# Weighting a mixture of experts at its inputs instead of its outputs, with one PSUM accumulator, in a two-layer transformer kernel

## The chip, the cores and the metric

The kernel runs on one core of a Trainium2 chip. A core has TensorE (PE, matrix multiplies into PSUM), VectorE (DVE), ScalarE (ACT, activation functions and copies), GpSimd (POOL) and SyncE (SP, which here only issues DMAs). SBUF is the working memory of 128 partitions. PSUM has eight banks of 128 partitions x 512 float32. The engines run at their own pace and wait on semaphores. The metric is the device time of one execution in microseconds (us), lower is better.

## What is computed

Two layers on `x` of 16 sequences x 256 tokens x 128 features. The first adds a linear-kernel attention and a two-deep local-attention network. The second, the one that the change is about, adds a 16-head softmax attention and a mixture of 8 experts with a shared one:

```python
xn = _layernorm(x)
x = x + _L1_attn_ref(xn, Wk, bk, Wq, bq, Wv, bv, Wo, bo) + _L1_ffn_ref(xn, ...)

# _L1_ffn_ref: E = 8 experts, K = 2 chosen, H = 256
logits = jnp.einsum('bsd,de->bse', x, Wr) * SCALE
_, idx = jax.lax.top_k(logits + rb, K)
w = jax.nn.softmax(jnp.take_along_axis(logits, idx, axis=-1), axis=-1)
w_full = jnp.sum(jax.nn.one_hot(idx, E, dtype=x.dtype) * w[..., None], axis=-2)
h = jnp.einsum('bsd,edh->bseh', x, W1) * jax.nn.silu(jnp.einsum('bsd,edh->bseh', x, W3))
expert_out = jnp.einsum('bseh,ehd->bsed', h, W2)
out = jnp.einsum('bsed,bse->bsd', expert_out, w_full)
hs = jnp.einsum('bsd,dh->bsh', x, Ws1) * jax.nn.silu(jnp.einsum('bsd,dh->bsh', x, Ws3))
return out + jnp.einsum('bsh,hd->bsd', hs, Ws2)
```

Both kernels compute all eight experts for every token; `w_full` is zero where an expert was not chosen.

## The kernel before

All weights are loaded once (`block.sync`). Then eight turns run, each on two sequences (T = 512 tokens). Most tiles are feature-major: 128 features on the partitions, 512 tokens along the row. Every engine has its own hand-written instruction list, and the order within a turn is the order of that list.

A turn: layer norm; first layer; `x1` (token-major) is its result; a second layer norm (`norm`, DVE) gives `xn`; four transposes and an ACT copy give `xn2T`. From there, which is called the second part of the turn below:

- PE multiplies `xn2T` by the query and key weights (L739), the router weights `wr` (L743, eight small passes) and the value weights (L749).
- Queries and keys are split in three bfloat16 parts (ACT L932, POOL L429, ACT L934, POOL L431), stored to DRAM (`dparts`, SP L367) and read back, rearranged, by 26 DMAs (`qst`, `kst`; SP L373, L378). The semaphore `stack_in` tells that they have landed.
- DVE adds a bias to the values (`avz`, L1192) and then works out the router's top-2 weights `wf` in some 25 small, linked steps (L1203 to L1229), with an Exp on ACT in their midst (L937).
- PE computes experts. `expert_in(e)` makes four 128x512 products (L773 gates with `mw3`, L776 units with `mw1`). ACT applies Silu to the gates (L942), and DVE multiplies (`expert_hidden`, L1241) into `mh`. `expert_out(e)` multiplies `mh` by `mw2` in eight 128x128 pairs of passes (L765) into a PSUM bank of its own. DVE then adds it to `moe`, each token times its weight (`expert_add`, four instructions, L1252).
- Three experts run ahead of the wait for `stack_in` (`EARLY = 3`). Then 16 pairs of heads have their score maxima taken (PE L791 into `att_max` banks, DVE L1262), with one expert after every third pair (`EXPERT_AT`). The negated maxima (L1269, L1270) are transposed (PE L802), copied by ACT (L945) and sent through DRAM into `qst` (SP L382, L386; semaphore `nm_in`).
- Meanwhile PE computes the shared expert's gates and units (`expert_in(EX)`). Then come the scores (L817), 32 Exps on ACT (L955) and the value products (L833).
- At the end DVE divides (L1276, L1278), PE runs the output projection and the shared expert's `mw2` products into one bank (`final`, L763, L765), DVE adds `moe` (L1282), and SP stores `res`.

PSUM banks are given out at build time by `job(name, k, freed_by, count)`, in the order of PE's list. Ring `short` goes round banks 0 to 5, `long` holds 6 and 7. `freed(name)` is the wait for the last user of the bank. DVE's linked steps (`link`) each wait for the one before. `rsqrt` (L1003 to L1012) is a bit trick and three Newton steps of four linked instructions. It runs six times a turn: in both layer norms, and in each of the two local layers once on 64 columns (`loc_rs`) and once for its own layer norm (`glu_rs`).

## Time and profile before

| | |
|---|---|
| median of 3 runs (lowest to highest) | 2773.8 us (2756.99 to 2775.79) |
| the profiled execution's own time | 2776.88 us |
| its span, first to last instruction | 2774.7 us |
| mean granted TensorE clock | 0.872 |
| busy: PE / DVE / ACT / POOL | 73% / 50% / 25% / 8% of the span |
| chain that ended last, by engine | PE 58%, DVE 23%, DMA 6%, ACT 5% |

The profile is one execution. Its chain of work is followed back from the last instruction, at each step to what released it. A wait "<- X" is idle time that ended when X finished. The granted clock is 1.00 at 2.4 GHz and 0.50 at 1.2 GHz; a mean between them is a mix of both. A matmul on float32 stands in the trace as two passes, so "x2" is one product.

### The profile page before, as it was taken

How to read it: one execution, taken by the hardware profiler on the slowest of the kernel's cores; microseconds unless marked ns; L12 is line 12 of the kernel's file. 1: busy time of each engine (PE TensorE's matmuls, PEld its weight loads, DVE VectorE, ACT ScalarE, POOL GpSimd, SP SyncE). 2: the span in 40 equal slices, each digit the busy share in tenths (PEclk: the TensorE clock that was granted, in tenths of full speed). 3: DMA queues.
4: the chain of work that ended last, by engine and by line, in shares of the span. 5: the costliest groups of instructions: out<-in, count | busy, mean ns of one | idle time of the engine just before them, and what ended most of it. 6: DMA issues, size and time to landing. Idle time of an engine off the chain costs nothing.

```text
span 2774.7 us, 46305 instructions
## 1 busy us (share of the span) xinstructions
PE 2017.6 (73%) x19416; PEld 1126.0 (41%) x19416; DVE 1386.3 (50%) x3418; ACT 698.5 (25%) x1241; POOL 227.9 (8%) x178
## 2 busy tenths in 40 slices
PE   2777777767777577876778767787677866768667
PEld 1434434334354333543435434344343443434434
DVE  2554635545365453554545545455445554455544
ACT  1222141221412214122241223322132221322113
POOL 1011010110101101011010110100101101011000
PEclk9987989879898798987989879898798987989789
DMA  3000100001000100001000010000200002000020
GB/s 136 2 1 1 35 10 2 1 18 19 8 2 1 25 12 9 2 1 28 8 9 2 1 31 6 8 2 1 35 2 8 2 1 35 2 9 2 1 35 6
DMA packets 33581, 35.99 MB, mean 13 GB/s; under 512 B 3600, under 2 KB 31936, under 8 KB 32832
## 3 DMA queue, kind: packets, MB, share of 16 engines
q1 hardware_dynamic: 33376, 33.04, 5.7%
q8 instruction: 155, 2.54, 0.4%
q14 instruction: 50, 0.41, 0.1%
HBM read 24.38 MB, written 8.65 MB: 12 GB/s over the span
## 4 chain that ended last, share of the span: by engine, by line
PE 58%; DVE 23%; DMA 6%; ACT 5%; issue 4%; SPq 3%; POOL 1%; POOLq 0%; ACTq 0%; DVEq 0%
PE bank L557 5%; PE bank L765 4%; PE bank L833 4%; PE bank L773 4%; PE bank L611 3%; PE bank L517 3%; PE bank L776 3%; DMA lc<-in_ones 3%; PE bank L549 3%; PE bank L645 3%; DVE lrec L1133 2%; DVE lmx L1119 2%; PE bank L685 2%; PE bank L569 2%; PE bank L712 2%
## 5 line engine op out<-in xcount | busy, mean ns | idle before, releaser
L765 PE MATMUL bank<-w_mw,mh 128*128 128x128 f32 x1152 | 165.3, 298 | 118.5 <-DVE mh L1241 118.5
L765 PEld LDWEIGHTS bank<-w_mw,mh 128*128 128x128 f32 x1152 | 151.6, 210 | 169.6 <-issue 142.8
L942 ACT ACTIVATE silu<-bank 128x512 f32<-128x512 f32 x128 | 75.5, 597 | 411.8 <-PE bank L773 411.7
L773 PE MATMUL bank<-xn2T,w_mw 128*128 128x512 f32 x288 | 173.9, 689 | 4.5 <-DVE amx L1262 0.7
L1133 DVE RECIPROCAL lrec<-bank 128x256 f32<-128x256 f32 x64 | 112.3, 1755 | 126.2 <-PE bank L658 125.6
L410 POOL TENSOR_TENSOR lc<-lc,ls 128x512 f32<-128x512 f32 x32 | 40.7, 1271 | 1627.9 <-DVE lc L1094 1627.9
L1262 DVE TENSOR_REDUCE amx<-bank 128x2 f32<-128x512 f32 x256 | 157.1, 681 | 13.5 <-PE bank L791 13.5
L776 PE MATMUL bank<-xn2T,w_mw 128*128 128x512 f32 x288 | 157.4, 629 | 0.0
L557 PE MATMUL bank<-hT,w_wqkv 128*128 128x512 f32 x256 | 139.1, 675 | 23.3 <-ACT hT L859 17.3
L1252 DVE SCALAR_TENSOR_TENSOR moe<-bank,route,moe 128x128 f32<-128x128 f32 x256 | 72.1, 345 | 154.3 <-PE bank L765 154.3
L1241 DVE TENSOR_TENSOR mh<-bank,silu 128x512 f32<-128x512 f32 x144 | 98.3, 687 | 88.2 <-PE bank L776 86.9
L1119 DVE TENSOR_REDUCE lmx<-bank 128x4 f32<-128x512 f32 x128 | 79.5, 684 | 63.6 <-PE bank L611 63.6
L457 PE MATMUL bank<-w_ident,xn 128*128 128x128 f32 x64 | 17.4, 428 | 127.6 <-DVE xn L1027 127.6
L1276 DVE RECIPROCAL xn<-bank 128x256 f32<-128x256 f32 x16 | 28.1, 1757 | 159.0 <-PE bank L833 159.0
L884 ACT ACTIVATE lsq<-bank 128x512 f32<-128x512 f32 x128 | 74.7, 597 | 129.1 <-PE bank L549 71.7
L1114 DVE TENSOR_TENSOR lc<-lc,bank 128x512 f32<-128x512 f32 x128 | 79.1, 678 | 37.8 <-PE bank L592 37.8
L903 ACT ACTIVATE lnmT<-bank 128x512 bf16<-128x512 bf16 x16 | 9.6, 597 | 341.7 <-PE bank L620 341.7
L776 PEld LDWEIGHTS bank<-xn2T,w_mw 128*128 128x128 f32 x288 | 61.2, 213 | 82.3 <-issue 69.2
L557 PEld LDWEIGHTS bank<-hT,w_wqkv 128*128 128x128 f32 x256 | 48.6, 210 | 108.5 <-issue 51.2
L645 PE MATMUL bank<-lc 32*128 32x192 f32 (+1 forms) x2048 | 91.9, 321 | 0.0
L611 PE MATMUL bank<-lc 32*64 32x128 f32 (+1 forms) x3072 | 90.0, 298 | 0.0
L685 PE MATMUL bank<-mh,w_wo 128*128 128x512 f32 x128 | 58.7, 601 | 37.8 <-DVE mh L1136 37.8
(222 smaller groups left out, 3765.4 us busy)
## 6 DMA issues: line engine op xcount, KB each, us to landing
dparts<-parts SPq DMA_DIRECT2D x8, 768.0 KB, 3.7
phi<-dparts SPq DMA_DIRECT2D x96, 64.0 KB
lc<-dparts SPq DMA_DIRECT2D x96, 64.0 KB
w_mw<-in_mw SPq DMA_DIRECT2D x3, 1152.0 KB, 13.6
x_in<-in_x SPq DMA_DIRECT2D x8, 256.0 KB, 3.0
out<-res SPq DMA_DIRECT2D x8, 256.0 KB, 2.4
w_wqkv<-in_wqkv SPq DMA_DIRECT2D x1, 1536.0 KB, 7.6
w_w<-in_w SPq DMA_DIRECT2D x1, 682.0 KB, 8.9
```

What stands on the lines that cost most here:

```text
L557: mm(bank_of("loc_raw", n)[:], W["wqkv"][:, l, c * P:(c + 1) * P], h, start=True, stop=True).then_inc(sem["loc_raw_ps"], 1)
L611: ins = mm(bank_of("loc_max", k + i)[u * WIN:u * WIN + m, c0:c0 + P], lc[r, c, q0 + u * WIN:q0 + u * WIN + m], lc[r, 4 + c, k0:k0 + P], st ...
L645: ins = mm(bank_of("loc_sT", 4 * k + i)[:, c0:c0 + nq], lc[r, 4 + c, t + kt * P:t + kt * P + P], lc[r, c, t + q0:t + q0 + nq], start=False ...
L685: last = mm(o[:], W["wo"][:, l, c, :], loT[:, c, :], start=(c == 0), stop=(c == 3))
L765: last = mm(o[:, t], mh[:, (2 * e + i) % 4, t], W["mw2"][:, e, i, :], start=(e < EX and i == 0), stop=(i == 1))
L773: mm(o[:], W["mw3"][:, e, i * P:(i + 1) * P], xn2T[:], start=True, stop=True).then_inc(sem["moe_g_ps"], 1)
L776: mm(o[:], W["mw1"][:, e, i * P:(i + 1) * P], xn2T[:], start=True, stop=True).then_inc(sem["moe_u_ps"], 1)
L833: last = mm(o[32 * j:32 * j + 32, den * SEQ:(den + 1) * SEQ], v, apr[(4 * quad + j) % 8][:, kt * SEQ:(kt + 1) * SEQ], start=(i == 0 and kt ...
L1119: V.tensor_reduce(lmx[:, :, h % 4, g], bank_of("loc_max", 8 * l + h)[:].rearrange("p (j k) -> p j k", j=TT), AX.X, ALU.max).then_inc(sem[" ...
L1133: V.reciprocal(lrec[:, k % 2, :], bank_of("loc_den", k)[:, 0:SEQ]).then_inc(sem["loc_rec"], 1)
L1241: V.tensor_tensor(mh[:, n % 4, :], bank_of("moe_u", n)[:], silu[:, n % 2, :], ALU.mult).then_inc(sem["moe_h"], 1)
L1262: V.tensor_reduce(amx[:, 2 * b:2 * b + 2, h], bank_of("att_max", n)[:].rearrange("p (t k) -> p t k", t=2), AX.X, ALU.max).then_inc(sem["at ...
```

## The change

1. **Weight at the input.** The router weight of an expert is multiplied into the input of its `mw1` product, `xn2T`, instead of into its output. To have the weight along the tokens of a feature-major tile, `wf` is split by DVE in three bfloat16 parts (`wf3`, four more linked steps), transposed by PE (four passes), copied by ACT (`wT`), and for each expert spread over 128 partitions by one PE product with a column of the new constant `pick` (`expert_weight`), copied to SBUF by ACT (`widen`), and multiplied with `xn2T` by POOL into one of two buffers (`xw`).
2. **One accumulator.** All nine experts' `mw2` products and the output projection go to one bank (`final`, bank 5) without a break. The 32 `L1252` instructions of a turn go. The other jobs of the second part go round banks 0 to 4 (ring `five`).
3. **Order.** The router's product comes ahead of the query and key products; DVE does the routing ahead of `avz`. The shared expert (`ORDER[0]`) runs first, since it needs no weight. `expert_out(q - 1)` comes after `expert_unit(q)`. The first five weighted `q` run ahead of the score maxima (the fifth without its out), `q` = 5, 6, 7 with 5, 5 and 6 pairs behind them (`MAX_AT`). The last expert's gates, units and outs lie behind the transposes of the maxima.
4. **Newton steps** have three instructions instead of four.

```diff
@@ bank plan @@
-        EARLY = 3
-        EXPERT_AT = {6 * (e - EARLY) + 5: e for e in range(EARLY, EX)}
-        RINGS = {"short": range(0, 6), "long": range(6, 8), "quad": range(0, 4), "norm": range(4, 8)}
+        ORDER = [EX] + list(range(EX))
+        MAX_AT = {5: range(0, 5), 6: range(5, 10), 7: range(10, 16)}
+        RINGS = {"short": range(0, 6), "long": range(6, 8), "quad": range(0, 4), "norm": range(4, 8),
+                 "five": range(0, 5), "acc": range(5, 6)}
+        wf3 = sb("wf3", [P, TT, 3, EX], BF16)
+        wT = sb("wT", [3 * EX, T], BF16)
+        wide_w = [lsq[:, 0, :], lsq[:, 1, :]]
+        xw = [xnT[:], xB[:]]
+    c["pick"] = (np.arange(3 * EX)[:, None] % EX == np.arange(EX)[None, :]).astype(b)
@@ block.gpsimd @@
+                for q in range(1, EX + 1):
+                    pool.wait_ge(sem["moe_w"], now("moe_w", q))
+                    if q >= 3:
+                        pool.wait_ge(sem["moe_u_ps"], now("moe_u_ps", 2 * q - 2))
+                    nc.gpsimd.tensor_tensor(xw[q % 2], xn2T[:], wide_w[q % 2], ALU.mult).then_inc(sem["moe_xw"], 1)
@@ block.tensor @@
-                for e in range(EARLY):
-                    expert_in(e)
-                    expert_out(e)
...
+                def expert_weight(q):
+                    pe.wait_ge(*freed("moe_w", q))
+                    pe.wait_ge(sem["route_T"], now("route_T", 1))
+                    mm(bank_of("moe_w", q)[:], W["pick"][:, ORDER[q]:ORDER[q] + 1].broadcast_to([3 * EX, P]), wT[:],
+                       start=True, stop=True).then_inc(sem["moe_w_ps"], 1)
+
+                def expert_unit(q):
+                    if q:
+                        pe.wait_ge(sem["moe_xw"], now("moe_xw", q))
+                    for i in range(2):
+                        n = 2 * q + i
+                        pe.wait_ge(*freed("moe_u", n))
+                        mm(bank_of("moe_u", n)[:], W["mw1"][:, ORDER[q], i * P:(i + 1) * P], xw[q % 2] if q else xn2T[:],
+                           start=True, stop=True).then_inc(sem["moe_u_ps"], 1)
+
+                def expert_out(q):
...
+                            last = mm(bank_of("final")[:, t], mh[:, (2 * q + i) % 4, t], W["mw2"][:, ORDER[q], i, :],
+                                      start=(q == 0 and j == 0 and i == 0), stop=False, skip_group_check=True)
...
+                expert_gate(0)
+                expert_unit(0)
+                pe.wait_ge(*freed("route_T"))
+                pe.wait_ge(sem["route_w"], now("route_w", 1))
+                o = bank_of("route_T").bitcast(BF16)
...
+                expert_weight(1)
+                for q in range(1, EX):
+                    expert_gate(q)
+                    expert_weight(q + 1)
+                    expert_unit(q)
+                    if q not in MAX_AT:
+                        expert_out(q - 1)
+                        continue
+                    for i, pair in enumerate(MAX_AT[q]):
+                        if pair == 0:
+                            pe.wait_ge(sem["stack_in"], now("stack_in", 26 * 16))
+                        att_max(pair)
+                        if i == 1:
+                            expert_out(q - 1)
...
-                expert_in(EX)
+                expert_gate(EX)
+                expert_unit(EX)
+                expert_out(EX - 1)
+                expert_out(EX)
                 pe.wait_ge(sem["nm_in"], now("nm_in", 32))
...
-                expert_out(EX)
+                for b in range(G):
+                    pe.wait_ge(sem["att_o"], now("att_o", b + 1))
+                    for j in (2 * b, 2 * b + 1):
+                        t = slice(j * P, (j + 1) * P)
+                        last = mm(bank_of("final")[:, t], ftT[:, t], W["aw"][:, 3, :], start=False, stop=True,
+                                  skip_group_check=True)
+                last.then_inc(sem["final_ps"], 1)
@@ block.scalar @@
+                def widen(q):
+                    act.wait_ge(sem["moe_w_ps"], now("moe_w_ps", q))
+                    if q >= 3:
+                        act.wait_ge(sem["moe_xw"], now("moe_xw", q - 2))
+                    A(wide_w[q % 2], bank_of("moe_w", q)[:], ACT.Copy).then_inc(sem["moe_w"], 1)
+
+                gates(0)
+                act.wait_ge(sem["route_T_ps"], now("route_T_ps", 1))
+                A(wT[:], bank_of("route_T")[0:3 * EX, 0:256].bitcast(BF16), ACT.Copy).then_inc(sem["route_T"], 1)
+                widen(1)
+                for q in range(1, EX):
+                    gates(q)
+                    widen(q + 1)
@@ block.vector @@
                     for i in range(3):
-                        link(V.tensor_tensor(t, a, y, ALU.mult))
+                        link(V.scalar_tensor_tensor(t, a, -0.5, y, ALU.mult, ALU.mult))
                         link(V.tensor_tensor(t, t, y, ALU.mult))
-                        link(V.tensor_scalar(t, t, -0.5, 1.5, ALU.mult, ALU.add))
+                        last = V.scalar_tensor_tensor(y, t, 1.5, y, ALU.add, ALU.mult)
                         if i < 2:
-                            link(V.tensor_tensor(y, y, t, ALU.mult))
-                    return V.tensor_tensor(y, y, t, ALU.mult)
+                            link(last)
+                    return last
...
-                V.tensor_tensor(wf, one, two, ALU.add).then_inc(sem["route_w"], 1)
-
+                link(V.tensor_tensor(wf, one, two, ALU.add))
+                rest = R[6]
+                link(V.tensor_copy(wf3[:, :, 0, :], wf))
+                link(V.tensor_tensor(rest, wf, wf3[:, :, 0, :], ALU.subtract))
+                link(V.tensor_copy(wf3[:, :, 1, :], rest))
+                V.tensor_tensor(wf3[:, :, 2, :], rest, wf3[:, :, 1, :], ALU.subtract).then_inc(sem["route_w"], 1)
...
-                def expert_add(e):
-
-                    dve.wait_ge(sem["moe_out_ps"], now("moe_out_ps", e + 1))
...
-                    for j in range(TT):
-                        ins = V.scalar_tensor_tensor(moe[:, j, :], bank_of("moe_out", e)[:, j * P:(j + 1) * P],
-                                                     wf[:, j, e:e + 1], moe[:, j, :], ALU.mult, ALU.add)
-                    ins.then_inc(sem["moe_acc"], 1)
...
+                for q in range(EX):
+                    expert_hidden(q)
+                    for pair in MAX_AT[q] if q in MAX_AT else ():
+                        for n in (2 * pair, 2 * pair + 1):
...
```

What PE issues in the second part, from the router on. L762 is the router, L768 and L772 queries, keys and values, L779 a gate, L794 a unit, L828 the transposes of the weights, L785 the spread of a weight, L804 a product with `mw2` after the change; L739, L743, L749, L773, L776 and L765 are their counterparts before. Before:

```order
L739 MATMUL bank<-xn2T,w_aw 128x512 [waits glu_hid,xn2T]
L739 MATMUL bank<-xn2T,w_aw 128x512 [waits glu_gate]
L743 MATMUL bank<-w_wr,xn2T 128x8 [waits glu_hid]
L743 MATMUL bank<-w_wr,xn2T 128x8 x3
...
L773 MATMUL bank<-xn2T,w_mw 128x512 [waits x1]
L776 MATMUL bank<-xn2T,w_mw 128x512 [waits xn2T]
L773 MATMUL bank<-xn2T,w_mw 128x512 [waits att_qk]
L776 MATMUL bank<-xn2T,w_mw 128x512 [waits att_qk]
L765 MATMUL bank<-w_mw,mh 128x128 [waits moe_h,route_l]
L765 MATMUL bank<-w_mw,mh 128x128 x7
L773 MATMUL bank<-xn2T,w_mw 128x512 [waits att_v]
```

and after:

```order
L794 MATMUL bank<-xn2T,w_mw 128x512 [waits att_qk]
L828 MATMUL bank<-w_ident,wf 24x128 [waits route_w,att_qk]
L828 MATMUL bank<-w_ident,wf 24x128 x3
L785 MATMUL bank<-wT,w_pick 128x512 [waits route_T,moe_silu]
L779 MATMUL bank<-xn2T,w_mw 128x512 [waits moe_silu]
L779 MATMUL bank<-xn2T,w_mw 128x512 [waits moe_h]
L785 MATMUL bank<-wT,w_pick 128x512 [waits route_T,moe_h]
L794 MATMUL bank<-xB,w_mw 128x512 [waits route_T,moe_xw]
L794 MATMUL bank<-xB,w_mw 128x512 [waits moe_w]
L804 MATMUL bank<-w_mw,mh 128x128 [waits moe_h,att_v]
L804 MATMUL bank<-w_mw,mh 128x128 x7
```

Before, an expert's `mw2` products stand right behind its own gates and units. Now the previous expert's do, and the units wait for `moe_xw` from POOL; the second gate of `q` = 1 waits for the first hidden tile (`moe_h`), whose bank it takes.

The same list between the score maxima (L817 after, L791 before), from `q` = 5 to the gates of `q` = 6, after:

```order
L794 MATMUL bank<-xB,w_mw 128x512 [waits moe_h]
L817 MATMUL bank<-lc,phi 128x256 [waits moe_silu,stack_in]
L817 MATMUL bank<-lc,phi 128x256 x3
L817 MATMUL bank<-lc,phi 128x256 [waits moe_h,moe_w]
L817 MATMUL bank<-lc,phi 128x256 x3
L804 MATMUL bank<-w_mw,mh 128x128 [waits moe_h]
L804 MATMUL bank<-w_mw,mh 128x128 x7
L817 MATMUL bank<-lc,phi 128x256 [waits att_mx,moe_h]
...
L779 MATMUL bank<-xn2T,w_mw 128x512 [waits att_mx] x2
```

The wait for `stack_in` stands behind six gates and units now (three before), and the maxima of five pairs lie between two experts instead of three. At the end of the turn PE has before (left of the next turn's first transposes):

```order
L763 MATMUL bank<-w_aw,ftT 128x128 [waits att_o,moe_h,att_p]
L765 MATMUL bank<-w_mw,mh 128x128 x2
L763 MATMUL bank<-w_aw,ftT 128x128
L765 MATMUL bank<-w_mw,mh 128x128 x2
L763 MATMUL bank<-w_aw,ftT 128x128
L765 MATMUL bank<-w_mw,mh 128x128 x2
L763 MATMUL bank<-w_aw,ftT 128x128
L765 MATMUL bank<-w_mw,mh 128x128 x2
```

and after:

```order
L898 MATMUL bank<-w_aw,ftT 128x128 [waits att_o]
L898 MATMUL bank<-w_aw,ftT 128x128
L898 MATMUL bank<-w_aw,ftT 128x128 [waits att_o]
L898 MATMUL bank<-w_aw,ftT 128x128
```

Eight of the twelve products have moved ahead of the scores, and the first two of the four that are left wait only for the first sequence.

## Rows read from the trace of the kernel before

**Rows 1.** Chain of waits, second turn, 590 to 725 us: start, length, what.
```profile
599.09 0.18 DVE rt L1009
599.29 0.17 DVE rs L1011
...
604.11 3.79 PE bank L739 x4
...
628.69 14.22 DMA lc<-in_ones
```

**Rows 2.** The same chain, between two experts of the maxima's stretch.
```profile
652.55 1.12 PE bank L773 x2
...
660.32 0.61 DVE amx L1262
...
660.97 1.12 PE bank L773 x2
```

**Rows 3.** The same chain, from the maxima's transposes to the turn's last addition.
```profile
687.58 0.38 PE bank L802 x4
...
694.38 2.07 ACT phi L955 x4
...
715.04 1.77 DVE xn L1276
...
721.59 0.70 DVE res L1282
```

**Rows 4.** Timeline, second turn: start, length, instruction, [idle before <- what ended it].
```profile
611.10 1.91 PE L773 MATMUL bank<-xn2T,w_mw 128*128 128x512 f32 x2
611.34 1.66 DVE L1192 TENSOR_TENSOR avz<-bank,w_rows 128x32 f32<-128x32 f32 x16 [9.15 <-PE bank L749]
...
613.07 2.12 POOL L431 TENSOR_TENSOR parts<-fqs,parts 128x1024 bf16<-128x1024 f32 x1 [1.17 <-ACT parts L934]
613.13 2.11 DVE L1206 TENSOR_TENSOR route<-route,w_rb 128x32 f32<-128x32 f32 x1
...
620.44 0.21 ACT L937 ACTIVATE rsm<-rsm 128x8 f32<-128x8 f32 x1
...
621.76 0.19 DVE L1229 TENSOR_TENSOR route<-route 128x32 f32<-128x32 f32 x1
...
624.12 3.75 PE L765 MATMUL bank<-w_mw,mh 128*128 128x128 f32 x16 [8.47 <-DVE mh L1241]
...
633.35 2.02 PE L765 MATMUL bank<-w_mw,mh 128*128 128x128 f32 x16 [0.88 <-DVE mh L1241]
635.21 1.02 PE L773 MATMUL bank<-xn2T,w_mw 128*128 128x512 f32 x2
636.07 1.02 PE L776 MATMUL bank<-xn2T,w_mw 128*128 128x512 f32 x2
...
642.96 0.83 PE L791 MATMUL bank<-lc,phi 48*128 48x256 bf16 x12 [1.25 <-DMA lc<-in_ones]
```

**Rows 5.** Timeline, second turn, the shared expert's last unit behind the maxima.
```profile
692.27 1.02 PE L776 MATMUL bank<-xn2T,w_mw 128*128 128x512 f32 x2
```

**Rows 6.** Groups by line, whole run: names, shapes, count | busy us, mean ns | idle before.
```profile
L942 ACT ACTIVATE silu<-bank 128x512 f32<-128x512 f32 x128 | 75.5, 597 | 411.8 <-PE bank L773 411.7
...
L791 PE MATMUL bank<-lc,phi 48*128 48x256 bf16 x512 | 44.8, 285 | 43.1 <-DVE moe L1252 25.3 <-DMA lc<-in_ones 17.7
...
L412 POOL TENSOR_TENSOR lc<-lc,xn2T 128x512 f32<-128x512 f32 x32 | 40.8, 1273 | 0.0
...
L1093 DVE TENSOR_TENSOR ls<-bank,rot 128x512 f32<-128x512 f32 x32 | 21.8, 682 | 3.2 <-PE bank L557 3.2
```

**Rows 7.** Waits, whole run: who waited for whom, us in total, times, longest.
```profile
PE bank L583 <- DVE lr L1106: 64.0, 16, 4.0
...
PE bank L704 <- DVE rs L1012: 33.9, 16, 3.6
```

**Rows 8.** Stretches of the second turn: us, busy PE, PEld, DVE, ACT, POOL, clock, DMA, GB/s.
```profile
643.00:687.00 44.00, 33.48 (x184) 18.86 (x184) 31.31 (x63) 5.97 (x10) 0.00 (x0) 1.00 0.00 1
```

More of the change, by code:

```diff
@@ L778, in _ @@
[L778 to L782 removed]
+                            last = mm(bank_of("final")[:, t], mh[:, (2 * q + i) % 4, t], W["mw2"][:, ORDER[q], i, :],
+                                      start=(q == 0 and j == 0 and i == 0), stop=False, skip_group_check=True)
+                    last.then_inc(sem["moe_out_ps"], 1)
@@ L783, in _, with att_max @@
+                def att_max(pair):
                     b, hh = divmod(pair, AH // 2)
```

168 lines of the change are left out of this document (76 added, 92 removed).

## The prediction

> **What bounds the kernel now.** I read the page first: PE is busy for most of the span, but the eight turns are not PE at its peak, so the question is which wait ends last in the part that is changed. For that I read the chain of waits through one turn (the second), then the timeline of the same stretch, and last the groups, the waits and the clock.
>
> All times below are counted from T = 604.11, when PE has `xn2T` and starts the second part [rows 1]. The reader should see four stretches there.
>
> - *T to T+38.9.* PE runs three experts. It starts the first at T+7.0, but its `mw2` products wait 8.47 us for DVE, since the routing stands ahead of the hidden tiles on DVE and its Exp ahead of the Silus on ACT [rows 4]. Then it waits another 1.25 us for the last of the rearranging DMAs, and starts the maxima at 642.96 (T+38.9) [rows 4]. Over the run that DMA wait comes to 17.7 us [rows 6].
> - *T+38.9 to T+83.5.* Maxima and five experts; the transposes L802 come at 687.58 [rows 3]. The chain repeats every 8.42 us, from 652.55 to 660.97, and it is serial: PE's gates and units, DVE's hidden tile, PE's eight pairs, DVE's four additions into `moe`, one maximum (0.61 us), PE again [rows 2]. Nothing overlaps, though the clock is 1.00 and PE is busy only 33.48 of 44 us, DVE 31.31 [rows 8].
> - *T+83.5 to T+90.3.* The shared expert's gates and units hold PE until 693.1, and the first Exp starts at 694.38 [rows 3, 5].
> - *T+90.3 to T+117.5.* 32 Exps, then from the last reciprocal (715.04) to the final addition (721.59) 6.55 us, most of it the twelve products on PE [rows 3].
>
> **Stretch one, after.** The router's eight passes are now ahead of queries and keys. That moves queries, keys and the whole DMA chain by what they cost, which I estimate at 1.6 us. It lets DVE route while ACT and POOL split, so the weights' first half is ready near T+6. But the Exp stands on ACT behind the split copies, and those end at T+10.5 (the last split product on POOL started at T+9.0 before [rows 4], plus 1.6). With its table load the Exp is done at T+12.0. From there the seven steps that took 621.95 - 620.65 = 1.3 us [rows 4], and four new ones at 0.2 to 0.22, make T+14.2. I add 0.6 us, because POOL is then still in its split product. The row shows the price: L1206, a 0.19 us step with two SBUF inputs, took 2.11 us and ended at 615.24, with POOL's product at 615.19 [rows 4]. So `route_w` comes at T+14.8, against T+17.8 before.
>
> The Trainium skill ("SBUF — State Buffer", section "SBUF: two separate sides") says of this that VectorE instructions with two SBUF inputs and GpSimd instructions hold a shared pair of ports exclusively, and the loser blocks for the whole instruction. By that rule the eight new POOL products block no hidden tile and no maximum, which have one input in PSUM; if only the row's length were known, one would have to fear it (a rival below). The trace agrees: L1093, PSUM times SBUF on DVE, takes its 0.68 us in the stretch in which POOL rotates [rows 6].
>
> Then, in series: four transposes 0.4 (as L802 [rows 3]), ACT's copy 0.6 (as a Silu of 597 ns [rows 6]), the spread product 0.4 (512 bfloat16 columns, as many as the four transposes have [rows 3]), `widen` 0.6, POOL 1.27 [rows 6], and hops: `xw(1)` at T+18.7. PE fills this with the gates of `q` = 1, at the half clock that follows its wait (sixteen passes took 3.75 us at 624.12 and 2.02 us at 633.35 [rows 4]): 1.7 us each, T+16.4 to T+19.8. The spread and the units end at T+21.9, the first `expert_out` at T+23.8. From there each `q` costs PE's own work: four products at 0.86 (635.21 to 636.07), eight pairs 1.86 (633.35 to 635.21) [rows 4], a spread 0.3: 5.6 us. ACT (three instructions, 1.8 us), POOL (1.27) and DVE (two tiles, 1.4) lie beside it, two experts ahead by the double buffers. Three times 5.6 and the gates and units of `q` = 5 (3.7) end at T+44.3. The DMAs land at T+38.9+1.6 = T+40.5, so they are no longer waited for.
>
> **Stretch two, after.** It holds three more sets of gates and units (`q` = 6, 7; 5 is done), three outs and 32 maxima. Counted from the end of a `q`'s units: DVE finishes the hidden tile at 0.75 and then has ten maxima, 6.1 us, to 6.9. PE issues two pairs, the previous out (done at 2.4) and the other three pairs as banks come free; the next gates need the sixth and seventh maxima (4.4, 5.0), the spread the eighth, the units the ninth and tenth (6.3, 6.9), so they end at 8.2. That is 8.2 us for five pairs and an expert, where 8.42 us bought three pairs and an expert. Twice 8.2, then 0.75 + 12 x 0.61 + 0.5 for the last block and the negation: 25.1. The transposes come at T+69.4 instead of T+83.5: **14.1 us gained**.
>
> **Stretch three, after.** Behind the transposes PE now has gates, units and two outs: 5.5 us as before (687.58 to 693.1 [rows 3, 5], part of it at half clock) and 3.7 at full clock, then the scores. The first Exp comes some 9.6 us behind the transposes, not 6.8: **2.8 us lost**.
>
> **Stretch four, after.** Five banks instead of six let PE run two pairs ahead of the Exps instead of three. PE's work for four Exps is about as long as the Exps, so I cost this at nothing; if the cover fails it is some tenths per group. From the last reciprocal: 1.77 + 0.44 + a hop + two tiles of projection 0.5 = 2.9, against 6.55 [rows 3]. Some of that turn's products ran at half clock, so I count **2.8 gained**, not 3.6.
>
> **Newton steps.** A step costs 0.20 us from start to start [rows 1]. Three fewer in each of six calls, all on the chain (PE waits 64.0 us and 33.9 us over the run for the four calls of the local layers [rows 7], the other two are the norms): 3.6 us a turn at the most. The fused form is not in the trace at this size. Below, it costs what a plain step does; above, 0.05 more six times a call leave 1.8. I take **3.0 gained**.
>
> **Sum.** 14.1 - 2.8 + 2.8 + 3.0 = 17.1 per turn. The second turn waited 1.25 us for the DMAs and the mean turn 17.7/8 = 2.2 [rows 4, 6], so 1.0 more: 18.1. Eight turns: 145 us. The profiled execution took 2776.88, 2.2 more than its span, and 0.1% more than the median. 2776.9 - 145 = **2632 us**.
>
> **Rivals.**
> - *The array stays at half clock longer.* In stretch one PE still waits from T+11.4 to T+14.8. If it then needs one more expert to get back to 2.4 GHz, 5.6 us of work doubles: gain 12.5 a turn, 2677 us. For it: the half clock after 624.12. Against: the stretch after holds more PE work in a row. 0.13.
> - *POOL is in the way.* Hidden tiles and POOL's products exclude each other: 1.27 x 8 = 10.2 us a turn in a chain, 2714 us. For it the 2.11 us row, against it L1093. 0.06.
> - *Better than counted.* The clock recovers at once and the half clock of stretch three goes: 4 us a turn, 2600 us. 0.12.
> - *Slower than before.* One mechanism: the finer mixture of short waits on PE between maxima keeps the array at half clock. The nine experts hold 9 x 5.3 = 48 us of full-clock work a turn. The gain is gone once 18/48 = 38% of it runs at half clock beyond what does now. Half of it would give 2776.9 + 8 x (24 - 18) = 2825 us. Against: the clock is 1.00 in the maxima's stretch though PE idles a quarter of it [rows 8]. 0.03.
> - *No effect*, because another wait that I don't see takes the gain: 0.03.
>
> The forecast has 0.63, on its own 2605 to 2665. The range has to reach over the first rival and most of the better case, so 2592 to 2690. About 1% is what a measurement can tell from no change. Faster by over 1% (below 2746): 0.94; within 1%: 0.03; slower: 0.03.
>
> **What would show it.** Right: no L1252; the maxima start near T+44 with no DMA wait; an expert every 5.6 us ahead of the maxima and every 8.2 us among them; the transposes near T+69; the first Exp 9 to 10 us behind them; under 3.3 us from the last reciprocal to the final addition; three steps of 0.2 per Newton round; hidden tiles of 0.69 us. Wrong: PE waiting for `moe_xw`; maxima slower than 0.61 us apart; a granted clock below 0.9 in stretch two; fused Newton steps near 0.25 us; a DMA wait at `stack_in`.

## The result, and the profile after

| | before | after |
|---|---|---|
| median (lowest to highest), 4 runs each | 2765.39 us (2756.89 to 2775.79) | 2643.41 us (2641.73 to 2644.58) |
| the profiled execution, its span | 2776.88, 2774.7 | 2643.78, 2641.7 |
| mean granted clock | 0.872 | 0.872 |

The ratio is 0.9557 with an interval of 0.9526 to 0.9589: 4.4% faster. The forecast was 2632 us in a range of 2592 to 2690. Parts 1 and 4 of the page after:

```profile
PE 2023.3 (77%) x19512; PEld 1115.3 (42%) x19512; DVE 1285.2 (49%) x3050; ACT 735.7 (28%) x1313; POOL 309.1 (12%) x242
...
PE 64%; DVE 24%; ACT 5%; issue 4%; DMA 1%; POOL 1%; SPq 1%; ACTq 0%; DVEq 0%
```

PE's share of the chain rose and DMA's fell from 6% to 1%, as far as a page can say it. The rest is read by stretch. Here is the mean turn, worked out from the timelines of all eight turns (T is PE's first instruction on `xn2T`, L762 after; maxima, transposes and Exp are their first starts; the end is the start of the final addition):

| us | before | after | gained | forecast |
|---|---|---|---|---|
| T to maxima | 39.1 | 46.1 | | |
| T to transposes | 84.5 | 71.9 | 12.6 | 15.1 |
| transposes to first Exp | 7.1 | 10.1 | -3.0 | -2.8 |
| first Exp to last reciprocal | 21.2 | 20.7 | 0.5 | 0 |
| last reciprocal to end | 5.9 | 3.0 | 2.8 | 2.8 |
| end to next T | 222.2 | 218.6 | 3.6 | 3.0 |
| a turn, and eight | | | 16.6, 133 | 18.1, 145 |

The forecast of 15.1 holds the 1.0 for the DMAs. The difference of the spans is 133.0. From T to the end, the turns of after take 104.5 to 106.2 us and those of before 115.4 to 122.0, so a single turn of before can stand some 3 us from this mean.

Chain of waits after, second turn (T = 586.86), from the gates of `q` = 1 to the gates behind the transposes: start, length, what. In all rows of gates (L779) and units (L794), "x4" is four passes, that is the two products of one expert.

```profile
603.41 3.71 PE bank L779 x4
...
607.65 2.48 PE bank L794 x4
...
617.65 1.72 PE bank L779 x4
619.37 0.32 PE bank L785
619.69 1.91 PE bank L794 x4
621.60 1.78 PE bank L804 x16
...
633.11 0.69 DVE mh L1311
633.80 3.60 DVE amx L1320 x6
...
637.45 1.98 PE bank L779 x4
...
658.79 0.58 PE bank L849 x4
659.37 3.71 PE bank L779 x4
```

Ahead of the maxima the chain is PE alone: from 617.65 to the next gates at 623.39 an expert takes 5.73 us, all of it products (1.72 + 0.32 + 1.91 + 1.78). Among the maxima it alternates: hidden tile, six maxima, then gates, spread and units, 8.59 us for five pairs and an expert. No addition and no `mw2` product is in it. Before, a round took 8.42 us for three pairs [rows 2], and three more links stood between its products and its maximum:

```profile
656.29 0.70 DVE mh L1241
...
657.13 2.04 PE bank L765 x16
...
659.19 1.13 DVE moe L1252 x4
```

The gates' four passes take 3.71 us at 659.37, behind PE's wait for the last maxima, and 1.98 at 637.45. Two stretches of this turn, the gates of `q` = 1 and a later expert (us, busy PE, PEld, DVE, ACT, POOL, clock, DMA, GB/s), show the two levels, 1.2 and 2.4 GHz:

```profile
603.30:607.60 4.30, 4.30 (x7) 1.29 (x6) 1.48 (x3) 1.64 (x3) 1.27 (x1) 0.50 0.49 76
617.65:623.40 5.75, 5.75 (x27) 3.33 (x26) 1.38 (x2) 1.68 (x3) 1.27 (x1) 1.00 0.57 82
```

Timeline after, same turn, where the router's weights come:

```profile
597.27 2.12 POOL L448 TENSOR_TENSOR parts<-fqs,parts 128x1024 bf16<-128x1024 f32 x1 [1.17 <-ACT parts L990]
...
598.81 0.59 DVE L1280 TENSOR_TENSOR rsm<-rsm 128x4 f32<-128x4 f32 x1 [5.80 <-ACT rsm L993]
...
601.47 0.58 PE L828 MATMUL bank<-w_ident,wf 128*24 128x128 bf16 x4 [5.06 <-DVE wf L1291]
```

PE waits 5.06 us for `route_w` and then runs the gates of `q` = 1 at half clock (the stretch from 603.30 above); in the timeline they take 3.65 to 3.78 us in every one of the eight turns. Groups of after, whole run:

```profile
L1311 DVE TENSOR_TENSOR mh<-bank,silu 128x512 f32<-128x512 f32 x144 | 98.9, 691 | 240.9 <-PE bank L794 240.6
L817 PE MATMUL bank<-lc,phi 48*128 48x256 bf16 x512 | 42.0, 272 | 25.6 <-DVE amx L1320 25.6
...
L1074 DVE SCALAR_TENSOR_TENSOR rt<-ra,rs 128x4 f32<-128x4 f32 (+2 forms) x144 | 26.5, 184 | 4.9
```

L817 answers to L791 of [rows 6]: no DMA wait any more, and DVE's additions are gone from its releasers. Hidden tiles take 691 ns beside POOL's products. And the waits that answer to [rows 7], 64.0 and 33.9 us there:

```profile
PE bank L606 <- DVE lr L1173: 53.1, 16, 3.3
...
PE bank L727 <- DVE rs L1076: 23.4, 15, 2.6
```

### The profile page after: what moved, and what is told of

Same layout as the page of the kernel before. It is cut to its first block, busy times and chain, and to the rows that moved or that the text cites. A ratio compares the mean times of both kernels' runs of the same rounds, so it can differ in the third digit from the quotient of the medians.

```text
span 2641.7 us, 46366 instructions
## 1 busy us (share of the span) xinstructions
PE 2023.3 (77%) x19512; PEld 1115.3 (42%) x19512; DVE 1285.2 (49%) x3050; ACT 735.7 (28%) x1313; POOL 309.1 (12%) x242
## 4 chain that ended last, share of the span: by engine, by line
PE 64%; DVE 24%; ACT 5%; issue 4%; DMA 1%; POOL 1%; SPq 1%; ACTq 0%; DVEq 0%
PE bank L779 6%; PE bank L794 5%; PE bank L580 5%; DVE amx L1320 4%; PE bank L883 4%; PE bank L634 4%; PE bank L540 3%; PE bank L804 3%; PE bank L572 3%; PE bank L668 3%; DVE lrec L1200 3%; PE bank L708 3%; DVE lmx L1186 2%; PE bank L592 2%; PE bank L735 2%
## 5 line engine op out<-in xcount | busy, mean ns | idle before, releaser
L427 POOL TENSOR_TENSOR lc<-lc,ls 128x512 f32<-128x512 f32 x32 | 40.7, 1272 | 1149.3 <-DVE lc L1161 1149.3
L779 PE MATMUL bank<-xn2T,w_mw 128*128 128x512 f32 x288 | 167.0, 710 | 1.8
L999 ACT ACTIVATE silu<-bank 128x512 f32<-128x512 f32 x144 | 85.1, 597 | 285.4 <-PE bank L779 285.3
L804 PEld LDWEIGHTS bank<-w_mw,mh 128*128 128x128 f32 x1152 | 136.7, 192 | 24.2 <-issue 24.2
L580 PE MATMUL bank<-hT,w_wqkv 128*128 128x512 f32 x256 | 127.1, 623 | 23.3 <-ACT hT L915 17.3
L804 PE MATMUL bank<-w_mw,mh 128*128 128x128 f32 x1152 | 141.4, 277 | 0.0
L708 PE MATMUL bank<-mh,w_wo 128*128 128x512 f32 x128 | 68.0, 680 | 38.2 <-DVE mh L1203 38.2
L634 PE MATMUL bank<-lc 32*64 32x128 f32 (+1 forms) x3072 | 96.8, 315 | 0.0
L572 PE MATMUL bank<-lsq,w_sumrow 128*32 128x512 f32 x256 | 81.8, 605 | 12.1 <-ACT lsq L940 12.1
L668 PEld LDWEIGHTS bank<-lc 32*128 32x128 f32 x2048 | 85.5, 207 | 0.0
L634 PEld LDWEIGHTS bank<-lc 32*64 32x64 f32 (+1 forms) x3072 | 73.1, 170 | 27.7 <-issue 21.8
```

What stands on the lines that cost most here:

```text
L572: last = mm(bank_of("loc_ss", l)[r0:r0 + 32, :], W["sumrow"][:, g, :], lsq[:, ab, :], start=(g == 0), stop=(g == 1), skip_group_check=True)
L580: mm(bank_of("loc_raw", n)[:], W["wqkv"][:, l, c * P:(c + 1) * P], h, start=True, stop=True).then_inc(sem["loc_raw_ps"], 1)
L634: ins = mm(bank_of("loc_max", k + i)[u * WIN:u * WIN + m, c0:c0 + P], lc[r, c, q0 + u * WIN:q0 + u * WIN + m], lc[r, 4 + c, k0:k0 + P], st ...
L668: ins = mm(bank_of("loc_sT", 4 * k + i)[:, c0:c0 + nq], lc[r, 4 + c, t + kt * P:t + kt * P + P], lc[r, c, t + q0:t + q0 + nq], start=False ...
L708: last = mm(o[:], W["wo"][:, l, c, :], loT[:, c, :], start=(c == 0), stop=(c == 3))
L779: mm(bank_of("moe_g", n)[:], W["mw3"][:, ORDER[q], i * P:(i + 1) * P], xn2T[:], start=True, stop=True).then_inc(sem["moe_g_ps"], 1)
```

## The experiments

The theory was a sum of separate gains: Newton steps 24 us, the earlier router some 3 us a turn, an out that is deferred and needs no additions. The runs had to show whether the parts are separate at all, and what holds the rest. Mean turns, read as above (medians in us; before ran at 2754 to 2767 us beside them). All ratios are to the kernel before. From T to the end the turns of before, e1, e7 and e8 differ among themselves by 6 to 8 us (e8: 128.7 to 135.0), those of e6 and x4 by about 3, all others by under 2:

| | T to maxima | to transposes | to Exp | T to end | end to T | median |
|---|---|---|---|---|---|---|
| before | 39.1 | 84.5 | 7.1 | 118.7 | 222.2 | 2765.4 |
| after | 46.1 | 71.9 | 10.1 | 105.7 | 218.6 | 2643.4 |
| e1 Newton only | 38.4 | 83.6 | 6.8 | 116.8 | 219.9 | 2740.4 |
| e2 no Newton | 46.1 | 71.9 | 10.2 | 105.7 | 222.9 | 2675.7 |
| e3 old router order | 50.0 | 75.8 | 10.0 | 109.5 | 218.3 | 2671.5 |
| e4 POOL twice | 46.2 | 71.9 | 10.1 | 105.7 | 218.6 | 2643.1 |
| e5 out not deferred | 54.9 | 87.5 | 8.7 | 119.9 | 218.7 | 2756.3 |
| e6 PE kept busy | 44.5 | 70.3 | 9.9 | 103.8 | 218.4 | 2623.5 |
| e7 before, deferred | 37.6 | 79.8 | 6.3 | 114.8 | 222.9 | 2744.5 |
| e8 additions later | 36.3 | 97.1 | 6.5 | 132.0 | 221.7 | 2875.7 |
| x3 maxima spread | 40.7 | 69.0 | 7.2 | 99.9 | 217.5 | 2592.3 |
| x4 spread and busy | 41.3 | 71.1 | 7.2 | 102.0 | 219.4 | 2615.9 |
| x3 again | 40.5 | 68.9 | 7.2 | 99.8 | 218.7 | 2596.3 |
| x5 out ahead | 42.3 | 72.0 | 7.2 | 102.9 | 218.5 | 2616.4 |

### e1 and e2: the Newton steps alone, and all but them

e1 is the kernel before with the three-instruction step; e2 is the changed kernel with the old one.

```diff
-                        link(V.tensor_tensor(t, a, y, ALU.mult))
+                        link(V.scalar_tensor_tensor(t, a, -0.5, y, ALU.mult, ALU.mult))
...
-                        link(V.tensor_scalar(t, t, -0.5, 1.5, ALU.mult, ALU.add))
+                        last = V.scalar_tensor_tensor(y, t, 1.5, y, ALU.add, ALU.mult)
...
```

> The kernel before with nothing but the Newton steps in three instructions. My theory: every one of the 18 steps that fall away per turn was on the chain at 0.20 us, so 8 x 18 x 0.195 = 28 us less than before, about 2737 us. Rival: the waits for the local layers' square roots are filled by other work; then only the two norms of a turn count, 8 x 6 x 0.195 = 9 us, about 2756 us.

> The kernel after with the Newton steps in four instructions as before. If the two parts add up, it is slower than after by what e1 is faster than before: 28 us by my theory, about 2671 us; 9 us by the rival.

e1: 2740.41 against 2766.78 us, ratio 0.9907 (0.9872 to 0.9942). e2: 2675.68, 32 us above after, ratio 0.9680 (0.9639 to 0.9721). So the steps are worth 26 to 32 us, alone or with the rest. Most of that lies outside the experts: e2's end to next T is 222.9 us against after's 218.6, and e1's 219.9 against before's 222.2. The rest of e1's gain is in the turn's second part, where its turns and those of before scatter too much to place it.

### e3: the router and its bias back behind the queries and keys

The router's product comes behind queries and keys on PE, and `avz` ahead of the routing on DVE, as before; the rest is after.

```diff
@@ block.tensor: the router's job and products moved behind these @@
+                for i in range(2):
+                    pe.wait_ge(*freed("att_qk", i))
+                    o = bank_of("att_qk", i)
+                    mm(o[:], W["aw"][:, i, :], xn2T[:], start=True, stop=True).then_inc(sem["att_qk_ps"], 1)
...
```

> The kernel after, with the old order at the start of the second part: queries and keys ahead of the router on PE, the values' bias ahead of the routing on DVE. My theory: the weights come at T+18.5 instead of T+14.5, and nothing hides that, since PE then waits for them: 4 us per turn, 32 us more than after, about 2675 us. Rival: the DMAs start 1.6 us earlier and PE has work for the shared expert only, so part comes back; 10 to 15 us more than after.

2671.45 us, 28 above e4's 2643.08 (which ran beside it and equals after), with the maxima 3.9 us later in every turn. Its timeline shows what it meets there:

```profile
600.39 2.12 POOL L448 TENSOR_TENSOR parts<-fqs,parts 128x1024 bf16<-128x1024 f32 x1 [1.17 <-ACT parts L990]
600.46 2.10 DVE L1273 TENSOR_TENSOR route<-route,w_rb 128x32 f32<-128x32 f32 x1
```

A 0.19 us step is held until POOL's product ends, as L1206 was in [rows 4]. After, one step too is held, L1280, but for 0.59 us instead of its usual 0.16. So some 1.5 us of the 3.9 are blocking that the new order removes. For the rest `avz`, 1.7 us of DVE [rows 4], is the nearest cause; it was not tried alone.

### e4: POOL does each of its new products twice

```diff
+                    pool.wait_ge(sem["pool_step"], now("pool_step", q + 1))
+                    nc.gpsimd.tensor_tensor(ls[:, 0, :], xn2T[:], wide_w[q % 2], ALU.mult).then_inc(sem["pool_step"], 1)
```

The second product goes to a tile that nobody reads.

> The kernel after, with POOL's product for each expert made twice (the first into a free buffer): 2.54 us of POOL per expert instead of 1.27. My theory: POOL is two experts ahead and shares nothing that the hidden tiles or the maxima need, so within 8 us of after. Rival (POOL is in DVE's way or in series with PE): 1.27 us for each of 64 experts, up to 80 us more, and DVE instructions that are longer than 0.70 us in the trace.

2643.08 us: no change for 81 us more of POOL's work. POOL's new products hold nothing up, which closes the rival "POOL is in the way"; its split product does hold one routing step (L1280). Hidden tiles take 691 ns here too. That agrees with the rule of the Trainium skill ("SBUF — State Buffer", section "SBUF: two separate sides") that the prediction drew on: steps with two SBUF inputs are held (L1273 above), hidden tiles, with one input in PSUM, are not.

### e5: the out not deferred

The changed kernel, but `expert_out(q)` stands right behind `expert_unit(q)` again; the shared expert's out goes ahead of the units of `q` = 1, and behind the transposes only the last expert's is left.

```diff
                     expert_unit(q)
+                    expert_out(q)
                     if q not in MAX_AT:
-                        expert_out(q - 1)
                         continue
...
-                        if i == 1:
-                            expert_out(q - 1)
...
```

> The kernel after, with each expert's mw2 products right behind its own units again (the shared expert's ahead of the units of q = 1). My theory: PE waits about 0.9 us for the hidden tile in each of eight experts, 7 us per turn, 56 us more than after, about 2700 us. Rival (the gain is that of the additions that fell away): within 10 us of after.

2756.32 us, 113 above after where 56 were expected, and almost back at the kernel before (ratio 0.9973, 0.9950 to 0.9996). Its chain, second turn:

```profile
649.97 0.70 DVE mh L1310
...
650.72 2.05 PE bank L804 x16
652.77 1.72 PE bank L779 x4
...
657.51 2.05 PE bank L804 x16
659.56 0.37 PE bank L817 x4
659.93 3.68 DVE amx L1319 x6
...
663.65 3.37 PE bank L779 x4
```

The turn is 14.2 us longer, where 7 were expected. Ahead of the maxima, hidden tile and out are in series with the rest: 6.79 us for an expert against 5.73, about the 0.9 that was expected, and one more out stands ahead of them, so that they start 8.8 us later. What was missed is the stretch of the maxima. There the six maxima that free the next gates' banks can't start until the out has run (0.70 + 2.05 + 0.37 us behind the units, with DVE idle), and PE, which idles while they run, then does the first gates at half clock (3.37 us). A block takes 12.75 and 11.14 us against 8.59. From maxima to transposes it is 32.6 us against 25.8. e1 ran beside e5, with the Newton steps alone, at 2740.41 us. So the weight at the input, the one accumulator and the new order, taken together but without the deferred out, are 16 us slower than the kernel before with the same Newton steps.

### e6: PE kept busy while it waits for the router

```diff
+                for i in range(4):
+                    mm(bank_of("route_T")[:], W["mw3"][:, 0, 0:P], xn2T[:], start=True, stop=True)
                 pe.wait_ge(sem["route_w"], now("route_w", 1))
```

Four products that nobody reads, in the bank of the transposes.

> The kernel after, with four products (3.4 us, overwritten by the transposes behind them) on PE ahead of its wait for the router's weights. My theory of the missing part of the gain: the wait of 5 us leaves the array at half clock for the next 7 us. With PE busy it stays at 2.4 GHz: gates, spread and units of q = 1 take 3.9 us instead of 7.3, so 3 us per turn, 24 us less than after, about 2619 us. Rival: the clock is half for another reason in this place (it is also half before the wait); then no change, or a little slower for the work added.

2623.47 us, 20 below after (ratio 0.9509, 0.9472 to 0.9546), mean clock 0.884. PE's gates of `q` = 1 in the second and third turn:

```profile
600.05 0.39 PE L830 MATMUL bank<-w_ident,wf 128*24 128x128 bf16 x4 [1.54 <-DVE wf L1293]
...
601.72 2.08 PE L779 MATMUL bank<-xn2T,w_mw 128*128 128x512 f32 x2
...
926.00 1.13 PE L779 MATMUL bank<-xn2T,w_mw 128*128 128x512 f32 x2
```

The rows of L779 are the first two passes of the gates: the same work behind the same waits (PE idle for 1.54 us here and there), at half clock in one turn and at full clock in the next. The filler itself ran at a clock of 1.00 in both. The first two turns take 46.4 us to the maxima, as after does (45.5 to 46.5), five others 43.6 to 43.7 and one 45.1. So the half clock behind the wait does cost 2.5 us a turn, and the filler removes it in five turns of eight and half of it in a sixth. What decides it in a turn is not shown here.

### e7 and e8: the kernel before with the out deferred

If a deferred out alone bought the gain, the weighting at the input would not be needed. e7 is the kernel before with `expert_out(e - 1)` and `expert_add(e - 1)` one expert later.

```diff
...
                         expert_in(EXPERT_AT[2 * pair + 1])
-                        expert_out(EXPERT_AT[2 * pair + 1])
+                        expert_out(EXPERT_AT[2 * pair + 1] - 1)
+                expert_out(EX - 1)
...
```

> The kernel before, with an expert's mw2 products (and its additions into moe) moved behind the next expert's gates and units; nothing else. My theory: what the old stretch of maxima lost was the series PE, hidden tile, PE, additions. Deferring alone breaks it: a period of 6.6 us instead of 8.42, five times, and about 0.9 us for two early experts, 10.8 us per turn, 86 us in all, about 2680 us. Rival: DVE's additions (72 us busy in the run) are what costs, and they are still there: then at most 20 us less than before.

2744.48 us, ratio 0.9920 (0.9892 to 0.9949): 22 us where 86 were expected; its rival ("at most 20") was nearer. Two views of it, the chain between two experts among the maxima and the group of the maxima's products:

```profile
656.02 1.80 PE bank L768 x16
657.85 1.13 DVE moe L1257 x4
658.97 0.61 DVE amx L1268
659.63 1.12 PE bank L776 x2
...
L795 PE MATMUL bank<-lc,phi 48*128 48x256 bf16 x512 | 47.0, 298 | 91.7 <-DMA lc<-in_ones 67.1 <-DVE moe L1257 24.6
```

The hidden tile left the chain (period 7.30 us instead of 8.42), but the additions did not: they stand in DVE's list between PE's out and the maximum that PE waits for. And the time that PE gained ahead of the maxima went to the DMAs: it now waits 67.1 us for them, where it was 17.7 [rows 6]. That is 49 us that the deferral freed and could not use. The changed kernel does not meet this wait; its PE has six experts' gates and units to run before it needs the DMAs, instead of three.

It is not what the sum missed, though: the sum asked for 1.8 us a turn ahead of the maxima and 1.5 came. From maxima to transposes it asked for 9.1 us a turn and 3.2 came (45.4 to 42.2 in the table). In the second turn the first block is 3.1 us off, since PE comes back from its 11.16 us of waiting for the DMAs at half clock (the first gate takes 2.00 us instead of 1.12); the next three are 0.7 off each, by the period of 7.30; and the last is 1.7 off, with the last expert's out and additions now ahead of the transposes.

e8 takes the additions out of the way, four maxima later in DVE's list. Its edit against e7:

```diff
                     if n in EXPERT_AT:
                         expert_hidden(EXPERT_AT[n])
-                        expert_add(EXPERT_AT[n] - 1)
+                    if n == 31 or n - 4 in EXPERT_AT and n < 31:
+                        expert_add(6 if n == 31 else EXPERT_AT[n - 4] - 1)
```

> Like e7_before_deferred (the kernel before with every expert's products with mw2 one expert later), but DVE makes the four additions of an expert into moe only four maxima behind the next expert's hidden tiles (the last two experts' at the end). Theory: in e7 the period among the maxima was 7.30 us instead of 8.42, because the four additions (1.13 us) still stood in DVE's list between PE's products and the maximum that frees the bank of the next gates. PE's own work of a period is four products 3.44, eight pairs 1.86 and three pairs of maxima 1.3 = 6.6 us, DVE's is 6.2. With the additions off the chain the period comes to 6.6 to 6.9 us, 0.4 to 0.7 less in each of five periods: 2 to 3.5 us a turn, so 16 to 28 us below e7, about 2722 us beside a kernel before of 2766. That is still some 75 us above the changed kernel, because PE's three stretches hold 32 more maxima-bound steps and the late router. Rival: it is DVE's hidden tile, not the additions, that holds the chain: the period stays at 7.3 and the time at e7's 2744 within 5 us.

2875.67 us, ratio 1.045 (1.0403 to 1.0496): wrong on both sides, since theory and rival had it faster than e7 or equal. Its chain, second turn:

```profile
658.26 1.88 DVE amx L1268 x3
660.14 1.04 DVE moe L1257 x4
...
661.93 2.01 PE bank L776 x2
```

The six banks go round in the order of PE's list. The last pair ahead of the next expert takes the bank in which the out waits for its additions, so PE stands still until four maxima and the additions have run, and comes back at half clock: the first gate (L776, two passes) takes 2.01 us instead of 1.12. A period is 11.3 to 12.5 us. PE waited 111.3 us over the run for the additions, 25.3 in the kernel before [rows 6]. So an expert's additions cost more than their 1.1 us on DVE: they hold a bank of the ring from the out until they have run, and in both places tried something waits for them, the next gates in e7 or the next pair in e8.

One rival stays untested. e7 and e8 have the old order, with three experts ahead of the DMAs and five blocks of maxima, so they do not separate the weighting at the input from the order. What the deferral would gain with the additions kept but six experts ahead of the DMAs and three blocks of maxima, no run shows.

### x3: the maxima spread more evenly

After's chain among the maxima is six maxima and an expert by turns. x3 puts four pairs behind each of `q` = 4, 5, 6, 7, and `expert_out(7)` among the last pairs instead of behind the transposes.

```diff
-        MAX_AT = {5: range(0, 5), 6: range(5, 10), 7: range(10, 16)}
+        MAX_AT = {4: range(0, 4), 5: range(4, 8), 6: range(8, 12), 7: range(12, 16)}
...
                         if i == 1:
                             expert_out(q - 1)
+                        if q == EX - 1 and i == 3:
+                            expert_out(q)
...
-                expert_out(EX - 1)
                 expert_out(EX)
```

> The kernel after, with four pairs of maxima behind each of q = 4, 5, 6, 7 instead of 5, 5, 6 behind 5, 6, 7, and the eighth expert's mw2 products among the last pairs instead of behind the transposes. My theory: PE's and DVE's work of a block are then nearer to each other (7.2 and 6.3 us); from the units of q = 4 to the negation 28.0 us instead of 31.6, and 1.8 us less ahead of the first Exp: 5.4 us per turn, 43 us, about 2600 us. Rival: the DMAs land at about T+40.1, and pair 0 comes at T+40.5, so that PE waits for them in some turns; then 20 to 30 us.

2592.33 us, 51 below after, ratio 0.9400 (0.9359 to 0.9440); on another chip 2596.27, ratio 0.9409 (below). Chain, second turn:

```profile
620.70 0.69 DVE mh L1312
621.39 2.40 DVE amx L1321 x4
...
623.83 1.98 PE bank L779 x4
...
626.13 1.93 PE bank L794 x4
...
649.36 1.91 PE bank L779 x4
```

A block has four maxima in series instead of six: 7.39 us. Over the turn 20 maxima are in series (4, 4, 4 and 8) where after has 24 (6, 6 and 12), so the transposes come at T+69.0 instead of T+71.9. And the first Exp comes 7.2 us behind them instead of 10.1. That is more than the 1.86 us of the out that was moved, since the gates behind the transposes take 1.91 us, where after they ran at half clock (3.71): the moved out fills part of PE's wait for the last maxima, 1.1 us of idle time where it was 3.1. The two edits, the four blocks and the moved out, were not tried one by one. This version beats both kernels.

### x4, x3 again and x5: what did not add up

x4 adds e6's filler to x3, and moves the out of `q` = 3 ahead of the first pair of maxima.

```diff
...
+                    if q == 4:
+                        expert_out(q - 1)
...
-                        if i == 1:
+                        if i == 1 and q > 4:
...
```

> x3_maxima_spread (maxima of four pairs each behind q = 4, 5, 6, 7; 2592 us) with two edits more: four products that nobody reads on PE ahead of the wait for route_w, as in e6, and the out of q = 3 ahead of the first pair of maxima instead of behind the second. Theory: the filler brings the array back to full clock earlier in six of eight turns (2.5 us each in e6), but the maxima can't start much ahead of the landing of the DMAs at T+40.1, where x3 starts at T+40.7. The out of q = 3 (1.86 us) fills that time and no longer stands among the maxima. So 1.9 + 0.6 us in six turns: 15 us below x3, about 2577 us, ratio about 0.934. Rival: the out among the maxima of q = 4 was covered by DVE's maxima, then only 0.6 us a turn is left and the time is 2587 us or more.

2615.92 us, ratio 0.9501 (0.9470 to 0.9531): 24 slower than x3's first run instead of 15 faster. x5 has the moved out without the filler, beside x3 once more on the same chip.

> x4 without its filler products: x3 with the out of q = 3 ahead of the first pair of maxima instead of behind the second. x4 came out at 2616 us against x3's 2592. Theory: the out ahead is what costs: the first pair starts 1.5 us later (T+42.3) and the gates of q = 5 still wait for the maxima on DVE, now with PE idle ahead of them and at half clock (2.98 us instead of 1.98), so this kernel is some 2 to 3 us a turn above x3 on the same chip: 16 to 24 us. Rival: the filler is what costs (a wait pattern that leaves the array slow later in the turn); then this kernel is within 5 us of x3.

> The kernel of x3_maxima_spread once more, beside the next one on one chip. If the stretches outside the experts (217.5 us from a turn's last addition to the next T in x3's first run, 218.2 to 220.4 in x4's) differ by the chip and not by the kernel, this run shows them near 219, a time of some 2605 us; if they belong to the kernel, 2592 us and 217.5 again.

x3 again took 2596.27 us (ratio 0.9409, 0.9379 to 0.9439), and x5 2616.37 (0.9490, 0.9467 to 0.9513), 20 above it. So the moved out is what costs. The filler brings nothing that the times show on top of it: x4 and x5 are within 1 us, on different chips. In x4's trace it shortens the second part by 0.9 us a turn (102.0 against 102.9), and the stretch outside is 0.9 longer. x3 with the filler but its out in place was not run. PE in x5's second turn, timeline:

```profile
627.11 0.39 PE L817 MATMUL bank<-lc,phi 48*128 48x256 bf16 x4 [0.66 <-DVE amx L1323]
628.30 0.39 PE L817 MATMUL bank<-lc,phi 48*128 48x256 bf16 x4 [0.80 <-DVE amx L1323]
628.81 3.19 PE L779 MATMUL bank<-xn2T,w_mw 128*128 128x512 f32 x4
```

In x3 the out stands between the pairs and fills exactly the time in which PE waits for maxima; the gates behind it take 1.98 us. Moved ahead, it delays the first pair by 1.8 us (T+42.3 against T+40.5) and leaves PE idle for 0.66 and 0.80 us. The gates' four passes then take 3.19 us. Stretches of x5, columns as above:

```profile
624.00:628.80 4.80, 3.24 (x33) 2.31 (x31) 3.23 (x6) 0.00 (x0) 0.36 (x1) 1.00 0.00 0
628.80:632.00 3.20, 3.19 (x5) 0.99 (x5) 2.34 (x4) 0.60 (x1) 0.00 (x0) 0.60 0.00 0
```

The clock was still 1.00 while PE idled, and fell to a mean of 0.60 in the gates that came after. The 1.8 us of delay and the 1.2 us that the gates take longer are about the 3.1 us by which the transposes come later (72.0 against 68.9). The expectation of x3 again asked about the stretch outside the experts: x3 again shows 218.7 us from end to next T, 1.2 more than its first run on the other chip, 8 us over the seven gaps between turns, and it comes in single turns (217.3 in some, 219.7 in others). It belongs to the run or the chip, not to the edit.

## Why the prediction was right, point by point

- **Stretches one and two, 15.1 forecast, 12.6 measured.** The mechanism is as put: e5 and e7 show that neither the deferred out on top of the old kernel nor the rest of the change without it does it. Which part of the rest the deferral needs, no additions or the new order, the runs do not separate. Mis-sized were three terms. `route_w` came at T+14.5 (14.8 forecast) and `xw(1)` at T+18.5 (18.7), but the first out ended at T+25.1 and not 23.8, mainly since the units of `q` = 1 ran at half clock too (2.48 us for what I took as 1.72); the gates and the spread ahead of them ended 0.7 later than counted. An expert took 5.73 us and not 5.6: the units' four passes take 1.91 us up to the out and not 1.72 (what the 0.19 is was not tried). A block of maxima took 8.59 and not 8.2, again a first product behind a wait at 1.12 and the longer units. Together they make the 2.5 us.
- **"The DMAs are no longer waited for."** Right: 17.7 us [rows 6] went to none. e7 shows how near it was: 67.1 us as soon as PE comes early.
- **Stretch three, -2.8 forecast, -3.0 measured.** Gates at half clock 3.71 us, as feared.
- **Exp stretch, 0 forecast, 0.5 gained.** Before, two turns took 22.3 and 23.2 us, after all take 20.7. e1, with six banks as before, takes 20.7 too, so it isn't the number of banks. It is the clock: in just those two turns the first value products ran at half clock. The first eight passes in the sixth turn:

```profile
2061.66 1.08 PE L833 MATMUL bank<-phi,avz 128*32 128x256 f32 x8 [0.37 <-ACT phi L955]
```

The same eight take 0.60 us at 2067.51. In those two turns PE had sat idle for 3.72 and 1.81 us just ahead of the scores; after, the two outs fill that wait and PE goes into the scores without a pause. e7 has such waits (1.53 to 2.01 us) and slow value products in all eight turns, which is why this stretch takes 22.4 us there. The wait alone does not settle it: one turn of e1 had 1.62 us and kept the full clock.
- **Stretch four, 2.8 and 2.8.** The chain's last links after are as in the sum:

```profile
689.60 1.77 DVE xn L1331
...
691.87 0.73 PE bank L898 x4
692.62 0.70 DVE res L1336
```

- **Newton steps, 3.0 forecast, 3.6 measured.** The fused step costs what a plain one does (184 ns for L1074), so the full 18 x 0.20 us came. The middle that I took between the bounds was too careful, and the trace of before had a row of it: L1214, the same form on 32 columns, takes 0.19 us at 616.39, as the plain L1212 ahead of it does. e1 and e2 lie on both sides of its 29 us: 26 and 32.
- **The rivals.** *Half clock longer* was priced at 5.6 us a turn; it came in part, 1.3 us of it (T+25.1 for T+23.8), and e6 puts the whole cost of that half clock at 2.5. *POOL in the way* is refuted by e4 and by hidden tiles of 691 ns, *no effect* and *slower* by the result. *Better than counted* did not come, but x3 shows that such a time (2592 us) was in reach by another order.
- **The total.** The forecast is 12 us a run too good: 145 against 133. It was made against a profiled execution 11.5 us above the median of before's four runs; after's own profiled execution stands at its median. So the medians differ by 122 us. That the forecast of 2632 us is only 11 off the 2643.4 is in part luck of the base: from the median of 2765.4 the same 145 us would have said 2620.

What the prediction did not see is how the parts hang together. It added up the gains of separate edits; e5 shows that one of them, the place of the outs in PE's list, carries 113 us of a change of 122. With the Newton steps' 32 and the router's 28 that is more than the whole, so the parts are no sum: each edit is worth what the others leave it.

## What to carry to other kernels

A product whose result another engine must pick up costs not only that engine's instructions: it holds a bank of the ring and a place in that engine's list. Products into an accumulator that PE finishes alone are free of both, and can be put where PE waits; where they are put still matters (x3 against x5, 20 us). When two engines alternate (here maxima and experts), count how many steps of the one stand in series ahead of the other per block, and try blocks in which that number is smaller (24 in after, 20 in x3); put real products between the small ones, where PE would wait, not ahead of them. Ask of each time gained what is late next: with the same deferral in the kernel before, PE waited 49 us more for the DMAs.

## What the runs showed of the hardware

- The granted clock behind the same wait differs from turn to turn. With filler ahead of the wait (e6), the first two passes of the gates of `q` = 1 took 2.08 us in one turn and 1.13 in the next. Without filler, after had the half clock there in every turn. The Trainium skill ("TensorE: Matmul & The Clock Gate", section "Part 1: The HAM clock gate (the "warmup" mystery)") says that the number of slow matmuls after a start varies with the run; e6 shows it vary from turn to turn of one run.
- In x5 the clock fell behind idle stretches of only 0.66 and 0.80 us between short products: the four gate passes there took 3.01 to 3.20 us in all eight turns instead of 1.98. Such stretches do not always bring it down: in e5, behind 0.66, 0.80 and 0.80 us, the gates took 3.24 to 3.49 us in the first block of every turn, and in the second block 1.98 in six turns and 3.42 in two.
- `scalar_tensor_tensor` with two operations takes as long as `tensor_tensor` with one: 162 ns on 4 columns, 166 on 8 and 225 on 64, a mean of 184 over the Newton steps.
- DVE steps with two SBUF inputs were held by one POOL product three times over, in three orders: L1206 for 2.11 us [rows 4], L1273 for 2.10, L1280 for 0.59.
